# Delta-rule recurrence: the order of ScalarE's square and its copies of the second round of the block solve

## The chip, the cores and the metric

One Trainium2 chip; the program runs on one of its cores. The metric is the device time of one execution in microseconds (us), smaller is better. A core has five engines that run side by side and wait for each other by semaphores: TensorE (PE), VectorE (DVE), ScalarE (ACT), GpSimd (POOL) and SyncE (SP), the last of which only issues DMAs here.

## What is computed

A post-layer-norm transformer block on x of 4 x 2048 x 256 in float32, with 4 heads of width 64. Its attention is a gated delta rule. Cut to the part around the change:

```python
q, k = l2norm(q), l2norm(k)
v, kb = v * beta, k * beta
A = tril(-(kb @ k.T), -1)              # per chunk
T = inverse(I - A)                     # the solve
u, w = T @ v, T @ kb
for i in chunks:                       # the recurrence
    attn = causal(q_i @ k_i.T)
    u_adj = u_i - w_i @ S
    o_i = q_i @ S + attn @ u_adj
    S = S + k_i.T @ u_adj
o = p0*fir_s(v) + p1*fir_m(v) + p2*fir_l(v) + p3*o + p4*v
o = rmsnorm(o) @ Wo.T
x = layernorm(x + o)
x = layernorm(x + ffn(x))
```

## The kernel before, in words

The kernel has four stages, one after the other: `project` (projections, convolution, Gram matrices of the keys), `weights_fir` (gates, FIR filters, and the inverses of the 32-wide diagonal blocks), `delta` (the recurrence, line 792) and `ffn` (line 1451). Only `delta` is touched.

`delta` works in 16 steps (STEPS) of 128 tokens for all 4 batches, so 16 pairs of batch and head are in work at once. The 128 x 128 triangular inverse that a step needs is put together from inverses of its 32-wide diagonal blocks (`ddiag`, `tdiag`, loaded by SP) in four rounds of small matmuls. A round is four groups; each goes to one of the four PSUM banks `R`, in turn, and is taken out by a copy or an addition on another engine:

- N: TensorE multiplies `lt` by `ddiag`; ScalarE copies the result to `nmat`.
- A: `nmat` by `tdiag`; ScalarE copies it to `r1` (96 x 384 a group). VectorE subtracts `r1` from `tdiag` (term A, L1244).
- B: `nmat` by `r1`; ScalarE copies it to `r2` (64 x 256 a group). VectorE adds `r2` (term B, L1246).
- C: `nmat` by `r2`; VectorE subtracts it straight from the bank (L1261).

These rounds are run for step t+1 while step t's own recurrence goes on, and the output side (transposes T, product with Wo W, residual and layer norm) for step t-1. The result `tt` is used in step t+1 in `solve` (L1063).

The order on each engine is written out by hand; each engine takes its instructions in that order.

TensorE (`step`, from line 1094): state products X (L1051), N rounds, transposes T (L1035), attention scores Q (L1016), solve (L1063), W (L1040), outputs (L1074, L1079), state update (L1088), then A, B and C rounds (L1032).

ScalarE (`step`, from line 1181): N copies, T copies (L1161), two copies of the solution `us` (L1189), edges of `tt` (L1166), the issue of a load of raw feed-forward weights (L1171), then the square of the outputs `osq` (L1194), which waits for `mixed`, then A copies and B copies. After the step the rounded weights are made (L1177) and their store is issued (L1179).

VectorE (`step`, from line 1340): scores (L1255), a check of the rounded weights (L1334), residual (L1306), output scaling `o` (L1278), state S (L1283), mixing (L1286, signals `mixed`), head sums of `osq` (L1290, waits for the square), layer-norm statistics (L1313), term A, sums of the statistics (L1321), term B, C evacuations (L1261), right side (L1270), head normalisation (L1297), layer norm (L1327).

GpSimd takes the head sums to the power -1/2 (L1422, L1424), and the layer norm's variances (L1428, L1431). SP loads step t+2 (L916 on) once step t's state update has been done.

The first N round needs a bank that VectorE's C evacuations of the step before empty, one bank each (`bank_free`):

```python
elif not isinstance(dve0, int) or dve0:
    pe.wait_ge(dve_out, dve0 - 3 + r)
```

Step 0 has no output side (no T, W, statistics); step 15, the last, has no rounds of the solve.

Of the kernel before, what the change touches and what calls it, by code (L numbers as in the profile page):

```python
# [791 lines left out]
def delta(nc, sems, io, keep):  # L792
# [5 lines left out]
    with st.ctx:  # L798
# [91 lines left out]
        with nc.Block() as block:  # L890
# [250 lines left out]
            def arrived(eng, seq, kind, g, round0):  # L1141

                r = next(i for i, x in enumerate(seq) if x[:2] == (kind, g))
                eng.wait_ge(round_ready, round0 + r + 1)
                return R[r % 4]

            def round_base(t):
                return base(t, len)

            @block.scalar  # L1150
            def _(act):
                def copy_rounds(kind, seq, round0):
                    for g in range(2 if kind == "T" else 4):
                        bank = arrived(act, seq, kind, g, round0)
                        c = slice(g * 4, g * 4 + 4)
                        rows, cols = REGION.get(kind, (slice(0, P), slice(0, P - CH if kind == "N" else P)))
                        if kind == "T":
                            dst = oT[:, g, :].rearrange("p (b n) -> p b n", b=BATCH)
                        else:
                            dst = {"N": nmat, "A": r1, "B": r2}[kind][rows, c, cols]  # L1160
                        nc.scalar.activation(dst, bank[rows, :, cols], ACT.Copy).then_inc(act_out, 1)  # L1161

                def edges(t, p):

                    for end in (slice(0, CH), slice(P - CH, P)):
                        last = nc.scalar.activation(tt[p][end, :, end], tdiag[p][end, :, end], ACT.Copy)  # L1166
                    last.then_inc(edges_done, 1)

                def raw_weights(c):
                    act.wait_ge(w_checked, c + 1)  # L1170
                    act.dma_start(wraw[:, :], io["ffn_w"][:, bass.ds(c * WCH, WCH)]).then_inc(wraw_in, 16)  # L1171

                def round_weights(c):

                    act.wait_ge(wraw_in, c * 16 + 16)
                    act.wait_ge(w_stored, c * 16)
                    nc.scalar.activation(wround[:, :], wraw[:, :], ACT.Copy).then_inc(w_rounded, 1)  # L1177
                    act.wait_ge(w_rounded, c + 1)
                    act.dma_start(io["wr_s"][:, bass.ds(c * WCH, WCH)], wround[:, :].bitcast(f32)).then_inc(w_stored, 16)  # L1179

                def step(t, p, seq, round0, pre, tail):

                    if pre:
                        copy_rounds("N", seq, round0)
                    if tail:
                        copy_rounds("T", seq, round0)
                    for i in range(2):
                        act.wait_ge(y_ready, t * 2 + i + 1)
                        nc.scalar.activation(us[:, 4 * i:4 * i + 4, :, :], Y[i][:, :, :, :], ACT.Copy).then_inc(u_done, 1)  # L1189
                    if pre:  # L1190
                        edges(t + 1, p)
                        raw_weights(t + 1)
                    act.wait_ge(mixed, t + 1)
                    nc.scalar.activation(osq[:, :, :, :], o[:, :, :, :], ACT.Square).then_inc(sq_done, 1)  # L1194
                    if pre:
                        copy_rounds("A", seq, round0)
                        copy_rounds("B", seq, round0)

                raw_weights(0)
                copy_rounds("N", PRE, 0)  # L1200

                act.wait_ge(d_zero, 4)
                act.wait_ge(r_zero, 2)
                copy_rounds("A", PRE, 0)
                copy_rounds("B", PRE, 0)
                edges(0, 0)
                round_weights(0)
                step(0, 1, PRE, NPRE, True, False)
                round_weights(1)
                with act.Fori(0, MID // 2) as i:  # L1210
                    for j in range(2):
                        t = i * 2 + 1 + j
                        step(t, j, FULL, round_base(t), True, True)
                        round_weights(t + 1)
                t = STEPS - 1
                step(t, 0, LAST, round_base(t), False, True)
                act.wait_ge(total_ready, 1)
                nc.scalar.activation(flag[:, :], X[0][0:1, 0, 0, 0:1], ACT.Copy).then_inc(flag_done, 1)
                copy_rounds("T", LAST, round_base(t) + len(LAST))
# [700 lines left out]
```

## Time and profile before

| | |
|---|---|
| median of 3 runs | 2437.59 us (2434.59 to 2437.62) |
| the profiled execution: its own time | 2435.2 us |
| its span | 2433.3 us |
| mean granted TensorE clock | 0.956 |
| busy: PE / DVE / ACT / POOL | 89% / 51% / 37% / 24% of the span |
| ACT osq (L1194), first and last start | 664.9 and 1074.2 us, 16 of them, 1056 ns each |
| ACT copies r1 and r2 (L1161) | 632.5 to 1051.7 us, 64 of each form |

Times of rows are us from the span's start. The timeline merges neighbouring instructions of one line into one row: its start, how long the merged piece lasts, engine, line, operation, the tiles written and read, the shape of one instruction, their count, and in brackets how long the engine had been idle before it and what ended that. PE rows' ends are modelled. A granted clock of 1.00 is 2.4 GHz and 0.50 is 1.2 GHz.

### The profile page before, as it was taken

How to read it: one execution, taken by the hardware profiler on the slowest of the kernel's cores; microseconds unless marked ns; L12 is line 12 of the kernel's file. 1: busy time of each engine (PE TensorE's matmuls, PEld its weight loads, DVE VectorE, ACT ScalarE, POOL GpSimd, SP SyncE). 2: the span in 40 equal slices, each digit the busy share in tenths (PEclk: the TensorE clock that was granted, in tenths of full speed). 3: DMA queues.
4: the chain of work that ended last, by engine and by line, in shares of the span. 5: the costliest groups of instructions: out<-in, count | busy, mean ns of one | idle time of the engine just before them, and what ended most of it. 6: DMA issues, size and time to landing. Idle time of an engine off the chain costs nothing.

```text
span 2433.3 us, 40589 instructions
## 1 busy us (share of the span) xinstructions
PE 2157.0 (89%) x15412; PEld 1855.9 (76%) x15412; DVE 1235.5 (51%) x1872; ACT 895.2 (37%) x1425; POOL 593.4 (24%) x416
## 2 busy tenths in 40 slices
PE   7887865655699999967999999999999999999998
PEld 6776754555588888855888888888888888888887
DVE  5776758896477777762323332333333333323332
ACT  4554530002233334313434443444344334433442
POOL 2555555896344444430000000000000000000000
PEclk9999987887799999987999999999999999999999
DMA  3558759787989989925000000000000000000000
GB/s 131 194 197 204 194 200 211 198 207 236 241 229 249 250 235 241 254 79 219 1 18 17 0 17 17 17 0 17 17 17 0 17 17 17 0 17 17 18 1 18
DMA packets 346603, 257.53 MB, mean 106 GB/s; under 512 B 281394, under 2 KB 315698, under 8 KB 336434
## 3 DMA queue, kind: packets, MB, share of 16 engines
q1 hardware_dynamic: 333682, 232.65, 35.1%
q10 hardware_dynamic: 12864, 24.12, 2.8%
q8 instruction: 36, 0.59, 0.1%
q14 instruction: 21, 0.17, 0.0%
HBM read 156.85 MB, written 99.88 MB: 106 GB/s over the span
## 4 chain that ended last, share of the span: by engine, by line
PE 52%; issue 1%; DVE 1%; ACT 0%; DMA 0%; SPq 0%; POOL 0%; DVEq 0%; ACTq 0%; POOLq 0%
PE B L1611 46%; PE O L1639 5%; PE T L1567 1%; DVE yb L1738 0%; ACT gate L1677 0%; DMA wr<-wr_s 0%; SPq L1500 0%; DVE stats L1769 0%; ACT L1677 0%; DVE z L1764 0%; DVE z L1760 0%; DVE z L1783 0%; POOL rstd L1819 0%; SPq L1514 0%; DVEq L1733 0%
## 5 line engine op out<-in xcount | busy, mean ns | idle before, releaser
L1611 PE MATMUL B<-act1l,wr 128*128 128x512 f32 x1024 | 398.4, 389 | 0.0
L1611 PE MATMUL B<-act1h,wr 128*128 128x512 f32 x1024 | 398.3, 389 | 0.0
L1611 PE MATMUL B<-act0h,wr 128*128 128x512 f32 x1024 | 398.3, 389 | 0.0
L1611 PE MATMUL B<-act0l,wr 128*128 128x512 f32 x1024 | 398.3, 389 | 0.0
L1691 ACT ACTIVATE yb<-B,scol 128x512 f32<-128x512 f32 x256 | 176.2, 688 | 581.0 <-PE B L1611 581.0
L1726 DVE TENSOR_TENSOR act0l<-yb,act0h 128x512 fp32r<-128x512 f32 x256 | 176.1, 688 | 377.9 <-ACT act0h L1694 375.7
L1816 POOL TENSOR_TENSOR rstd<-mv,ln_eps 128x4 f32<-128x4 f32 x16 | 3.2, 199 | 1309.2 <-DVE mv L1777 1309.2
L379 DVE SCALAR_TENSOR_TENSOR acc<-proj,taps,acc 128x512 f32<-128x512 f32 x288 | 214.4, 750 | 92.3 <-ACT acc L334 83.7
L1726 DVE TENSOR_TENSOR act1l<-yb,act1h 128x512 fp32r<-128x512 f32 x128 | 88.6, 692 | 295.5 <-ACT act1h L1694 295.5
L224 PE MATMUL proj<-xt,w_qkv 128*128 128x262 f32 x768 | 195.0, 400 | 35.9 <-DMA xt<-in_xt 19.4
L1611 PEld LDWEIGHTS B<-act1h,wr 128*128 128x128 f32 x1024 | 192.2, 188 | 39.9
L1611 PEld LDWEIGHTS B<-act0h,wr 128*128 128x128 f32 x1024 | 192.2, 188 | 39.9
L1611 PEld LDWEIGHTS B<-act0l,wr 128*128 128x128 f32 x1024 | 192.2, 188 | 39.9
L1611 PEld LDWEIGHTS B<-act1l,wr 128*128 128x128 f32 x1024 | 192.2, 188 | 39.9
L1611 PE MATMUL B<-xh,wr 128*128 128x512 f32 x512 | 202.7, 396 | 11.8 <-DMA wr<-wr_s 7.6
L613 PE MATMUL conv<-toe,win 128*128 128x192 f32 x512 | 139.2, 433 | 83.1 <-DMA win<-v_s 41.8
L1611 PE MATMUL B<-xl,wr 128*128 128x512 f32 x512 | 200.8, 392 | 0.0
L613 PEld LDWEIGHTS conv<-toe,win 128*128 128x128 f32 x512 | 127.8, 316 | 94.4 <-DMA win<-v_s 43.0
L224 PEld LDWEIGHTS proj<-xt,w_qkv 128*128 128x128 f32 x768 | 141.5, 192 | 72.2 <-DVE acc L379 28.6
L1738 DVE SCALAR_TENSOR_TENSOR yb<-B,scol,gate 128x512 f32<-128x512 f32 x128 | 94.8, 750 | 183.7 <-ACT gate L1677 128.1
L783 POOL TENSOR_TENSOR two<-prods 128x256 f32<-128x256 f32 x64 | 123.6, 1932 | 17.7 <-DVE prods L725 17.7
L1611 PEld LDWEIGHTS B<-xh,wr 128*128 128x128 f32 x512 | 97.0, 189 | 37.7 <-DVE yb L1738 10.1
(164 smaller groups left out, 3477.6 us busy)
## 6 DMA issues: line engine op xcount, KB each, us to landing
qk_s<-yT SPq DMA_DIRECT2D x16, 1024.0 KB, 5.8
kk_s<-kfull SPq DMA_DIRECT2D x16, 1024.0 KB, 3.9
qk<-qk_s SPq DMA_DIRECT2D x16, 1024.0 KB, 6.7
lt<-kk_s SPq DMA_DIRECT2D x15, 1024.0 KB, 5.3
wraw<-in_ffn_w ACTq DMA_DIRECT2D x16, 704.0 KB, 6.4
wr_s<-wround ACTq DMA_DIRECT2D x16, 704.0 KB, 9.5
toe<-in_firp SPq DMA_DIRECT2D x64, 160.0 KB, 3.6
xt<-in_xt SPq DMA_DIRECT2D x16, 524.0 KB, 4.0
```

The source lines that it names most:

```text
L224: last = nc.tensor.matmul(proj[cb % 2][:, 2 * half:2 * half + 2, 0:XW], w_qkv[:, k, cb * P:cb * P + P], xt[p][:, k, 2 * half:2 * half + 2, ...
L379: nc.vector.scalar_tensor_tensor(out=acc[cb % 3][:, :, :], in0=proj[cb % 2][:, :, j:j + P], scalar=taps[:, cb, j:j + 1], in1=acc[cb % 3][: ...
L613: last = nc.tensor.matmul(conv[n % 2][:, c // 2, c % 2 * NF * WIN:(c % 2 + 1) * NF * WIN], win[h % 2][:, :, g * FCH + c], toe[part % 2][:, ...
L783: nc.gpsimd.tensor_tensor(two[n % 2][:, :, :], part[:, 0, :, :], part[:, 1, :, :], ALU.add).then_inc(two_done, 1)
L1567: last = nc.tensor.transpose(T[:, k, b * P:b * P + P], x1[p][:, b, k * P:k * P + P], ident)
L1611: last = nc.tensor.matmul(B[slot % 4][:, :], w, part, start=(k == 0 and i == 0), stop=(k == kts - 1 and i == len(parts) - 1))
L1639: last = nc.tensor.matmul(O[:, b, :], sets[0][i][:, k, b * P:b * P + P], wr[:, W3 + k * D:W3 + k * D + D], start=(k == 0 and i == 0), stop ...
L1691: last = nc.scalar.activation(dst, B[slot % 4][:, :], ACT.Gelu, scale=scol[:, slot:slot + 1])
L1726: nc.vector.tensor_tensor(sets[s][1][:, m, :], yb[n % 3][:, :], sets[s][0][:, m, :].bitcast(f32), ALU.subtract).then_inc(lo_done, 1)
L1738: nc.vector.scalar_tensor_tensor(out=dst, in0=B[(2 * m + 1) % 4][:, :], scalar=scol[:, HT + m:HT + m + 1], in1=gate[m % 2][:, :], op0=ALU. ...
L1816: nc.gpsimd.tensor_tensor(rstd[:, :], mv[:, :, 1:2].rearrange("p b o -> p (b o)"), ln_eps[:, :], ALU.add).then_inc(rs_link, 1)
```

## The change

ScalarE's A copies stand ahead of the wait for `mixed` and of the square; the B copies stay behind it. `pre` is true in steps 0 to 14.

```diff
                     if pre:
                         edges(t + 1, p)
                         raw_weights(t + 1)
+                    if pre:
+                        copy_rounds("A", seq, round0)
                     act.wait_ge(mixed, t + 1)
                     nc.scalar.activation(osq[:, :, :, :], o[:, :, :, :], ACT.Square).then_inc(sq_done, 1)
                     if pre:
-                        copy_rounds("A", seq, round0)
                         copy_rounds("B", seq, round0)
```

## Rows read from the trace of the kernel before

**Rows 1.** Page, chain that ended last, by line:
```profile
PE B L1611 46%; PE O L1639 5%; PE T L1567 1%; DVE yb L1738 0%; ACT gate L1677 0%; DMA wr<-wr_s 0%; SPq L1500 0%; DVE stats L1769 0%; ACT L1677 0%; DVE z L1764 0%; DVE z L1760 0%; DVE z L1783 0%; POOL rstd L1819 0%; SPq L1514 0%; DVEq L1733 0%
```
**Rows 2.** Timeline of PE, 863 to 896 us, one steady step and the next N:
```profile
863.94 3.81 PE L1032 MATMUL R<-ddiag,lt 128*128 128x96 f32 x32 [0.44 <-DVE tt L1261]
867.59 1.04 PE L1035 MATMUL R<-const,o 128*128 128x128 f32 x8
...
870.54 2.09 PE L1063 MATMUL Y<-x,tt 128*64 128x64 f32 x64
...
881.29 2.96 PE L1032 MATMUL R<-tdiag,nmat 128*96 128x96 f32 x32
885.67 3.18 PE L1032 MATMUL R<-r,nmat 128*64 128x64 f32 x64 [1.42 <-ACT r L1161]
...
891.26 3.81 PE L1032 MATMUL R<-ddiag,lt 128*128 128x96 f32 x32 [0.35 <-DVE tt L1261]
```
**Rows 3.** Windows: stretch, its length, busy PE, PEld, DVE, ACT, POOL, PEclk, DMA share, GB/s:
```profile
868.00:895.00 27.00, 25.18 (x375) 23.56 (x374) 19.49 (x38) 10.24 (x20) 12.60 (x7) 1.00 0.93 245
```
**Rows 4.** Timeline of DVE, 862 to 892 us:
```profile
881.40 1.40 DVE L1283 TENSOR_TENSOR S<-S,Y 64x512 f32<-64x512 f32 x2
882.84 1.22 DVE L1286 TENSOR_TENSOR o<-o,mix 128x1024 f32<-128x1024 f32 x1
885.18 1.22 DVE L1290 TENSOR_REDUCE ss<-osq 128x16 f32<-128x1024 f32 x1 [1.12 <-ACT osq L1194]
...
887.63 1.80 DVE L1244 TENSOR_TENSOR tt<-tdiag,r 96x768 f32<-96x768 f32 x2
...
890.93 0.87 DVE L1261 TENSOR_TENSOR tt<-tt,R 32x128 f32<-32x128 f32 x4
```
**Rows 5.** Timeline, 622 to 672 us, A round of the prologue:
```profile
631.51 2.93 PE L1032 MATMUL R<-tdiag,nmat 128*96 128x96 f32 x32
...
634.47 2.38 ACT L1161 ACTIVATE r<-R 96x384 f32<-96x384 f32 x5 [0.19 <-PE R L1032]
```
**Rows 6.** Timeline of ACT, the same steady step; 885.43 from a narrower stretch:
```profile
867.79 0.49 ACT L1161 ACTIVATE nmat<-R 128x384 f32<-128x384 f32 x1 [0.40 <-PE R L1032]
868.23 1.09 ACT L1161 ACTIVATE oT<-R 128x512 f32<-128x512 f32 x2
...
884.09 1.06 ACT L1194 ACTIVATE osq<-o 128x1024 f32<-128x1024 f32 x1 [9.67 <-DVE o L1286]
885.06 3.08 ACT L1161 ACTIVATE r<-R 96x384 f32<-96x384 f32 x8
885.43 1.23 ACT L1161 ACTIVATE r<-R 96x384 f32<-96x384 f32 x3
```
**Rows 7.** Timeline of DVE and PE, end of step 0 and of step 2:
```profile
670.28 0.87 DVE L1261 TENSOR_TENSOR tt<-tt,R 32x128 f32<-32x128 f32 x4
671.47 3.71 PE L1032 MATMUL R<-ddiag,lt 128*128 128x96 f32 x32
...
727.34 3.81 PE L1032 MATMUL R<-ddiag,lt 128*128 128x96 f32 x32 [1.52 <-DMA tdiag<-t_s]
```
**Rows 8.** Timeline of PE behind longer idle times, and one window (columns as rows 3):
```profile
396.26 3.80 PE L613 MATMUL conv<-toe,win 128*128 128x192 f32 x16 [2.09 <-DVE prods L725]
...
449.12 4.91 PE L613 MATMUL conv<-toe,win 128*128 128x192 f32 x16 [2.26 <-DMA toe<-in_firp]
...
450.50:453.70 3.20, 3.20 (x12) 3.10 (x11) 3.17 (x3) 0.00 (x0) 3.12 (x3) 0.50 1.22 228
...
645.18 6.94 PE L1032 MATMUL R<-ddiag,lt 128*128 128x96 f32 x32 [5.62 <-DMA tdiag<-t_s]
...
1058.12 1.97 PE L1035 MATMUL R<-const,o 128*128 128x128 f32 x8 [3.36 <-DVE o L1297]
1060.02 2.69 PE L1063 MATMUL Y<-x,tt 128*64 128x64 f32 x64
```
**Rows 9.** Tile tdiag, its DMAs from issue to landing:
```profile
DMA to landing us min/median/max: 2.4/4.3/6.9
```

## Prediction, made before the changed kernel had run

> **What bounds the kernel now.** I read the chain that ended last first. Its shares, 46% and 5% and then 1% and less, belong to lines 1567 and later, the feed-forward part [rows 1]. No line of the recurrence, in which the changed line stands, is in it, so the recurrence's bound must be read from its own timelines. It repeats itself: N rounds start at 863.94 and at 891.26, so a step is 27.32 us [rows 2], at a granted clock of 1.00 [rows 3].
>
> Follow one step. TensorE works almost without a gap from the N rounds (863.94) through the state update to the A rounds, which start right behind it (881.29): 17.35 us [rows 2]. Then VectorE has the lead: state 881.40, mixing 882.84 to 884.06, a wait of 1.12 for ScalarE's square, the head sums at 885.18, statistics, term A at 887.63, term B, and the C evacuations at 890.93 [rows 4]. The next N round starts 0.33 after the first C evacuation starts, because it needs the bank that this one empties; its 0.35 of idle time is put down to DVE tt [rows 2, 4]. So 17.35 + 9.97 = 27.32: the step is TensorE's part and VectorE's part in series, and **the square lies on the path**: VectorE is in order and stands in head_sums until it is done. TensorE's own wait for the first A copy (1.42, [rows 2]) is not on the path: without it N would still wait for the C evacuations.
>
> **The change part by part.** Nothing is added or removed. In steps 0 to 14 four A copies move ahead of the wait for the mixing and of the square; B copies stay behind it. No DMA issue is moved past anything but the square and the A copies: the raw-weight load is issued before both, the rounded-weight store after both. Step 15 has no A round.
>
> *When the copies can run.* The A matmuls start at 881.29 and take 2.96 [rows 2]. The fourth copy cannot start before its group is done. In the prologue the copies follow TensorE directly: matmuls from 631.51, fourth copy at 634.47, 2.96 later [rows 5]. So here 881.29 + 2.96 = 884.25 (884.29 with the 0.04 of the fourth N copy, 867.79 against 863.94 + 3.81 [rows 2, 6]).
>
> *When the square runs.* It now follows that copy. Queued A copies start 0.37 apart (885.06, 885.43), an N copy and the next one 0.44 (867.79, 868.23) [rows 6]. That puts the square at 884.62 to 884.73 against 884.09 now, which is just behind the mixing's end [rows 4, 6]. **The delay is 0.53 to 0.64; I take 0.59**, between the two, since the last A copy is like the first row in shape and like the second in having just waited.
>
> *What it costs on the path.* Everything in VectorE's queue from the head sums on starts 0.59 later. Terms A and B don't wait: the A copies end by 884.8 and the B copies, as worked out below, by 887.1, both before term A alone begins (887.63 and 0.59). Nothing on VectorE gets shorter, so the C evacuations and N are 0.59 later. Behind the last changed step there is no N; there TensorE's transposes (1058.12) wait for the normalisation (DVE o L1297), which stands in the same queue [rows 8]. GpSimd's power and the later layer norm move along with VectorE.
>
> *What TensorE gains.* B starts right behind A, 1.42 earlier. The B copies wait for the square: first at about 884.66 + 0.97 = 885.63 (the present spacing of square and first copy [rows 6]), last done near 887.1, which leaves the C rounds and the state products about 1.4 earlier than now. They are worth nothing: the gap ahead of N becomes 0.35 + 1.42 + 0.59 = 2.36, in one piece. The cover of that gain is the C evacuation; if it went, TensorE would be next.
>
> *Two steps differ.* In step 0 there is no statistics work, and N (671.47) begins 1.19 after the C evacuation (670.28), right behind the state products [rows 7]. There the products come earlier, and N starts at 670.28 + 0.59 + 0.33 = 671.20: a gain of 0.27. In step 2 N waited 1.52 for the diagonal blocks' DMA, 1.17 more than the usual 0.35 [rows 7]; that hides 0.59. The load is issued after the state update, which doesn't move. So 15 changed steps make 13 x 0.59 - 0.27 = **7.4 us**.
>
> *Contention.* The A copies now read PSUM while VectorE adds the state and mixes; no row shows the two side by side. The low end is 0. For the high end let them take turns, with the mixing late by four whole copies, 4 x 0.37 = 1.5 a step, from the spacing above. I take 0: the nearest rows are the present A copies beside the head sums, which take 1.22, the same as the mixing with nothing beside it [rows 4, 6].
>
> *The clock.* A gap of 2.36 is longer than any in the steady stage. Elsewhere, after 2.09 idle the convolution's 16 matmuls took 3.80 (237 ns each), after 2.26 idle 4.91 (307 ns each), and the granted clock behind the latter was 0.50, its lower level of 1.2 GHz. After 3.36 idle TensorE's rows are longer too: transposes 1.97 and solve 2.69, where the steady step has 1.04 and 2.09, 0.93 + 0.60 = 1.53 lost [rows 2, 8]. After 5.62 idle N took 6.94 for 3.81, 3.13 lost [rows 2, 8]. So a fall costs 1.53 to 3.13 on TensorE's part, which is on the path. The low end of the number of falls is 0 (behind 1.52 N took its usual 3.81, [rows 2, 7]), the high end 13. At 2.36, just over the gap that fell, I take 5 of 13 at 1.53, the row nearest to the gap: **7.6 us**.
>
> The Trainium skill (TensorE: Matmul & The Clock Gate, "What's actually happening") says that the slow clock is the default and that activity alone releases it. By that rule gathering two short pauses into one long one speaks against this change, and the sum would be 15.0; by the gaps of 2.09 and less alone it would be 7.4.
>
> **Sum.** The profiled execution took 2435.2 (span 2433.3 and 1.9 around it). 2435.2 + 7.4 + 7.6 = 2450.2. The median of the runs, 2437.59, is 2.4 above that execution, so the forecast is 2452.6.
>
> **Rivals.** About 0.2% (4.9 us) is what a measurement of this kernel can tell from no change.
>
> (a) *No fall of the clock.* 7.4 alone: 2445.0. For it: 2.09 did nothing. Against: 2.26 did.
>
> (b) *The clock falls in every step.* 13 x 1.53 + 7.4 = 27.3: 2464.9; at 3.13 each 48.1: 2485.7. For it: the gap is the same in each step. Against: it lies between a row that kept the clock and one that lost it.
>
> (c) *Not slower: the DMA of the diagonal blocks is the real gate of N.* It is issued behind the state update, in several parts, and each takes 2.4 to 6.9 to land, median 4.3 [rows 9], while N starts 9.97 behind the update [rows 2]. A step in which it lands 0.59 or more behind the C evacuation hides the delay; from 5 further such steps on the total of (a) is under 4.9, and with all 13 it is 2437.3. Against: 0.33 from evacuation to N in the steady steps, and only step 2 shows a DMA. The same result would come if the copies didn't hold up the square at all, that is if the fourth A group were done by 883.7; the prologue's 2.96 speaks against it.
>
> (d) *Faster.* TensorE's 1.4 would count if N did not wait for VectorE. All 13 together would be 18 less, 2419. The 0.33 speaks against it.
>
> **How the numbers follow.** Some falls 0.44, none 0.28, nearly all 0.18, (c) 0.08, (d) 0.02. The first case spans 2446 to 2464. The range 2443 to 2470 takes in (a) with its 0.53 to 0.64 (6.6 to 8.0, some 1.5 of scatter between runs) and the cheap half of (b); outside are (c), (d) and the dear half of (b). Faster 0.02, same 0.08, slower 0.90.
>
> **What would show it.** Right: ACT osq starts about 0.6 after DVE's mixing ends, and DVE's wait for it grows from 1.12 to about 1.7; TensorE's wait of 1.42 ahead of B is gone and the one ahead of N is near 2.4, put down to DVE tt; undisturbed steps of 27.9; a clock under 1.00 in some of the steps, with N, T or Q rounds longer there. Wrong: a square at 884.1 behind the A copies, a wait for N put down to DMA in most steps, a step that shrinks. If the clock stays at 1.00 everywhere, the second term falls; if it falls in every step, the count was too small.

## The result and the profile after

| | before | changed |
|---|---|---|
| median | 2436.09 us (2431.0 to 2437.62, 4 runs) | 2461.06 us (2453.03 to 2461.6, 4 runs) |
| profiled execution / its span | 2435.2 / 2433.3 us | 2461.6 / 2459.8 us |
| ratio to before | | 1.0098, 95% interval 1.0072 to 1.0125 |

The changed kernel is slower by 1.0%, some 24 us, with the forecast at 2452.6 and the range from 2443 to 2470. Run once more beside others (`after_again`, below) its ratio was 1.0097 (1.0082 to 1.0113). Lines below the edit have moved by one: L1290 of before is L1291 after, and the square is L1196.

The page of the changed kernel, its heading and the granted clock in the 40 slices:

```profile
span 2459.8 us, 40589 instructions
PE 2172.0 (88%) x15412; PEld 1869.0 (76%) x15412; DVE 1241.5 (50%) x1872; ACT 899.6 (37%) x1425; POOL 583.0 (24%) x416
...
PEclk9999977887799999997999999999999999999999
```

The same number of instructions, and TensorE busy for 15 us more (2157.0 before): the same matmuls took longer. The page can't say which. The windows view over the middle of the recurrence can. Its columns are those of [rows 3]; first the kernel before, then the changed one:

```profile
680.00:1040.00 360.00, 334.82 (x4910) 313.58 (x4906) 264.35 (x498) 137.57 (x263) 164.55 (x93) 1.00 0.94 241
```
```profile
680.00:1040.00 360.00, 328.79 (x4664) 308.66 (x4664) 253.63 (x465) 131.16 (x246) 147.04 (x87) 0.96 0.90 228
```

In the same 360 us 246 fewer TensorE instructions were done, at a granted clock of 0.96 in place of 1.00. So there are two things: TensorE stands idle for longer in each step, and its clock is slower for part of the time. The timeline of one step, and of the N round behind it, TensorE first, answers to [rows 2]:

```profile
899.90 2.96 PE L1032 MATMUL R<-tdiag,nmat 128*96 128x96 f32 x32
902.79 3.30 PE L1032 MATMUL R<-r,nmat 128*64 128x64 f32 x64
906.29 2.02 PE L1051 MATMUL X<-S,qk 128*128 128x128 f32 x16 [0.20 <-issue]
910.58 3.81 PE L1032 MATMUL R<-ddiag,lt 128*128 128x96 f32 x32 [2.27 <-DVE tt L1262]
...
938.60 5.44 PE L1032 MATMUL R<-ddiag,lt 128*128 128x96 f32 x32 [2.51 <-DVE tt L1262]
```

The 1.42 ahead of the B round is gone, and the pause ahead of N has grown from 0.35 to 2.27 and 2.51, still put down to VectorE's C evacuations. The step, from N round to N round, is 938.60 - 910.58 = 28.02 for 27.32. And the second N took 5.44 for 3.81. VectorE and ScalarE in the same step answer to [rows 4, 6]:

```profile
900.01 1.40 DVE L1284 TENSOR_TENSOR S<-S,Y 64x512 f32<-64x512 f32 x2
901.45 1.23 DVE L1287 TENSOR_TENSOR o<-o,mix 128x1024 f32<-128x1024 f32 x1
904.49 1.22 DVE L1291 TENSOR_REDUCE ss<-osq 128x16 f32<-128x1024 f32 x1 [1.82 <-ACT osq L1196]
...
910.25 0.87 DVE L1262 TENSOR_TENSOR tt<-tt,R 32x128 f32<-32x128 f32 x4
```
```profile
902.89 0.49 ACT L1161 ACTIVATE r<-R 96x384 f32<-96x384 f32 x1 [0.19 <-PE R L1032]
903.40 1.06 ACT L1196 ACTIVATE osq<-o 128x1024 f32<-128x1024 f32 x1
904.37 1.16 ACT L1161 ACTIVATE r<-R 64x256 f32<-64x256 f32 x4
```

The fourth A copy starts 2.99 after the A round, the square 0.51 after that, and VectorE waits 1.82 for it where it waited 1.12: **0.70 late**. From the head sums on VectorE does what it did before: C evacuation 5.76 after the head sums (5.75 before), N 0.33 after that. And the granted clock in a window inside that second N round (938.60 to 944.04), 0.50:

```profile
940.60:943.80 3.20, 3.20 (x17) 3.20 (x17) 2.17 (x5) 0.98 (x2) 0.00 (x0) 0.50 1.04 400
```

In this way N rounds of 5.43 or 5.44 stand in 6 of the steps and one of 6.80 in a seventh:

```profile
734.59 5.43 PE L1032 MATMUL R<-ddiag,lt 128*128 128x96 f32 x32 [3.27 <-DMA tdiag<-t_s]
879.57 6.80 PE L1032 MATMUL R<-ddiag,lt 128*128 128x96 f32 x32 [2.51 <-DVE tt L1262]
```

A step that begins with a long N is 29.65, one that begins with a normal N 28.02: a fall costs 1.63. The one of 6.80 begins a step of 31.01: 2.99. In the six cases of 5.43 or 5.44 the clock went down 1.1 to 1.9 us after N had started; in the one of 6.80 it was at 0.50 already when N started. The length of the pause doesn't tell which N will be long: of the six pauses of 2.51 two are followed by a long N, of the five of 2.27 three.

**The sum of the profile.** To keep what comes before the recurrence out, I take the stretch from the N round of the second solve (645.18 before, 649.76 after) to the transposes of the last step (1058.12 and 1084.88): 412.94 and 435.12, 22.2 more. It comes apart as 13 steps x 0.70 = 9.1 (all but steps 0 and 2); the falls 6 x 1.63 + 2.99 = 12.8; step 2, at whose end a DMA gates N, 0.6 beyond its fall; step 1 0.4 beyond its 0.70; step 0 shorter by 0.6. That is 22.3. The entry itself lay at 643.5 to 650.1 in the fourteen profiles, in no order that follows the change (649.76 and 643.71 in two profiles of the changed kernel), and I take it for scatter.

### The profile page after: what moved, and what is told of

Read it like the earlier page. It is cut to its first block, busy times and chain, and to the rows that moved or that the text cites. A ratio compares the mean times of both kernels' runs of the same rounds, so it can differ in the third digit from the quotient of the medians.

```text
span 2459.8 us, 40589 instructions
## 1 busy us (share of the span) xinstructions
PE 2172.0 (88%) x15412; PEld 1869.0 (76%) x15412; DVE 1241.5 (50%) x1872; ACT 899.6 (37%) x1425; POOL 583.0 (24%) x416
## 4 chain that ended last, share of the span: by engine, by line
PE 51%; issue 1%; DVE 1%; ACT 0%; DMA 0%; SPq 0%; POOL 0%; DVEq 0%; ACTq 0%; POOLq 0%
PE B L1612 46%; PE O L1640 5%; PE T L1568 1%; DVE yb L1739 0%; ACT gate L1678 0%; DMA wr<-wr_s 0%; SPq L1501 0%; DVE stats L1770 0%; ACT L1678 0%; DVE z L1765 0%; DVE z L1761 0%; DVE z L1784 0%; POOL rstd L1820 0%; SPq L1515 0%; DVEq L1734 0%
## 5 line engine op out<-in xcount | busy, mean ns | idle before, releaser
L1032 PE MATMUL R<-ddiag,lt 128*128 128x96 f32 x512 | 78.4, 326 | 68.3 <-DMA tdiag<-t_s 39.5
L1032 PEld LDWEIGHTS R<-ddiag,lt 128*128 128x128 f32 x512 | 75.8, 239 | 71.6 <-DVE tt L1262 36.6
```

Of the source, the lines that this page charges most:

```text
L1032: last = nc.tensor.matmul(out, left, right, start=True, stop=True)
```

## Experiments

Two terms were to be told apart, and rivals that name the DMAs. Every run was timed against the kernel before on its chip; "stretch" is the length defined above (412.9 before, 435.1 changed).

### Fill the pause: fill16, fill8, fill4

The edit on TensorE, with n = 16, 8 and 4:

```diff
                     from_state(t, p)
+                    if seq is FULL:
+                        for j in range(n):
+                            nc.tensor.matmul(Y[1][:, j % 4, :, :], ident, ident, start=True, stop=True)
                     run("N", *rest)
```

> The changed kernel with 16 matmuls of 128x128 added on TensorE between the state products and the N rounds of steps 1 to 14 (their results go to a free bank and are read by nobody). They take about 2.05 us and fit in the wait of 2.27 to 2.51 ahead of N. Theory (two terms: the square is 0.70 late on VectorE in each step; the one long pause lets the clock fall, 7 times in the profile, 12.8 in all): steps of 28.02, granted clock 1.00 throughout steps 1 to 13, N always 3.81; the second term goes and the first stays, about 2436.1 + 13 x 0.70 = 2445. Rival (the loss is late DMAs or contention, and the clock only goes along with it): TensorE is as late as before, 2461 or above. Rival (the pause is no pause, N is held by TensorE itself): each step longer by 2, about 2489.

Measured: 2471.66, ratio 1.0139 (1.0122 to 1.0156). I had mis-sized the filler. One of these float32 matmuls is two instructions in the trace, and 16 of them take 3.74, not 2.05:

```profile
875.09 3.74 PE L1100 MATMUL Y<-const 128*128 128x128 f32 x32
878.66 3.60 PE L1032 MATMUL R<-ddiag,lt 128*128 128x96 f32 x31
```

N comes without any wait (the row shows 31 of its 32 instructions), TensorE gates it, and the steps from the third on are 28.81 to 29.06. The 2445 of the theory was missed; the rival's 2461 or above is met, but by the filler's length and not by what the rival named. The run doesn't weigh the terms, though it shows what was wanted of the clock: there is no fall in steps 1 to 14, and every N has its normal length. The run with 8 was the one that fitted.

> As the run with 16, with 8 such matmuls, about 1.05 us, so that a pause of 1.2 to 1.5 is left ahead of N. Theory: the kernel before has pauses of 1.42 and 1.52 without a fall, so the clock stays at 1.00 here too: again about 2445. If any pause beside the shorter work before it lets the clock fall, some falls stay and the time lies between 2445 and 2461.

Measured: 2447.17, ratio 1.0042 (1.0029 to 1.0055), stretch 421.3:

```profile
866.79 1.95 PE L1100 MATMUL Y<-const 128*128 128x128 f32 x16
869.47 3.81 PE L1032 MATMUL R<-ddiag,lt 128*128 128x96 f32 x32 [0.72 <-DVE tt L1265]
```
```profile
680.00:1040.00 360.00, 350.95 (x5045) 330.38 (x5046) 269.36 (x489) 136.53 (x256) 151.52 (x91) 1.00 0.93 234
```

Steps 1 to 13 are 28.02 (28.01 to 28.03), the clock is 1.00. The pauses left are 0.23 to 0.72, shorter than the 1.2 to 1.5 of the expectation, so what it says of such pauses is not tested here. TensorE does more work than in the changed kernel and the program is 14 us faster. This parts the loss: about 10 us (7 to 13) is the late square, the rest, 13.6 by the two ratios, went with the long pause. By their intervals the 13.6 has some 7 us either way (13.4, and 5 either way, with `after_again` below). The falls counted in the profile come to 12.8.

> The changed kernel with 4 matmuls ahead of N (two rows of the trace each, about 1.0 us by the 1.95 that 8 took), which leaves a pause of 1.2 to 1.5. Theory: no fall of the clock with such a pause, steps of 28.02, the same 2447 as with 8. Rival (any pause that stands alone ahead of N lets the clock fall): falls in some steps, 2450 to 2460.

Measured: 2452.57, ratio 1.0072 (1.0059 to 1.0086). A miss for the theory as I had put it. The pauses left are 1.38 and 1.62, one of 2.60 by a DMA, and three N rounds are long, each behind a pause of 1.62:

```profile
818.06 5.44 PE L1032 MATMUL R<-ddiag,lt 128*128 128x96 f32 x32 [1.62 <-DVE tt L1265]
875.73 3.81 PE L1032 MATMUL R<-ddiag,lt 128*128 128x96 f32 x32 [1.62 <-DVE tt L1265]
```

So a pause as short as 1.62 can do it here, in 3 of 7 cases, and a fall costs the same 1.63. The 1.52 of [rows 7] was one case and proved less than I took from it. The three falls are 4.9; the medians of this run and of the one with 8 differ by 5.4. That these agree is in part chance, for the two profiles differ by 9.7 in the stretch (431.0 and 421.3), and 4.8 of that is no fall behind a pause: a slower clock in step 0 (1.9), a wait of 1.56 for DMA qk in step 1, and the wait of 2.60 in step 2.

### Undo the late square alone: three_first

ScalarE takes three A copies ahead of the square and the fourth behind it:

```diff
                     if pre:
-                        copy_rounds("A", seq, round0)
+                        copy_rounds("A", seq, round0, range(3))
                     act.wait_ge(mixed, t + 1)
                     nc.scalar.activation(osq[:, :, :, :], o[:, :, :, :], ACT.Square).then_inc(sq_done, 1)
                     if pre:
+                        copy_rounds("A", seq, round0, range(3, 4))
                         copy_rounds("B", seq, round0)
```

> Three of the four A copies ahead of the square, the fourth behind it. The third group is done at about 2.2 into the A round, and its copy's slot ends as the mixing does. Theory: the square is not late (VectorE's wait for it is 1.12 again), steps of 27.32, the first term is gone; TensorE still runs early, with a pause of about 1.8 ahead of N. With no fall at 1.8: 2435 to 2437, same as the kernel before. Rival (TensorE's early B and C rounds and the pause alone cost the time): falls in several steps, N of 5.4 in them, 2436 + 1.6 each, up to 2450. Rival (the copies beside VectorE's state and mixing slow these down): VectorE's rows L1284 and L1287 above 1.40 and 1.23.

Measured: 2442.84, ratio 1.0025 (1.0016 to 1.0035), stretch 418.3; the time expected, 2435 to 2437, missed. The first term is gone as expected:

```profile
917.26 0.49 ACT L1161 ACTIVATE r<-R 96x384 f32<-96x384 f32 x1 [0.19 <-PE R L1032]
917.77 1.06 ACT L1196 ACTIVATE osq<-o 128x1024 f32<-128x1024 f32 x1
918.73 1.68 ACT L1161 ACTIVATE r<-R 96x384 f32<-96x384 f32 x5
```
```profile
918.86 1.22 DVE L1292 TENSOR_REDUCE ss<-osq 128x16 f32<-128x1024 f32 x1 [1.14 <-ACT osq L1196]
```

VectorE's wait is 1.14, and eight of the steps are 27.33 or 27.34. VectorE's mixing and state take 1.22 and 1.40 beside the copies, so there is no contention that these rows show. But it isn't quite the kernel before. Its pause is 1.71 to 1.84, without a fall behind any of those, and two N rounds, where a DMA or a late evacuation had made the pause 3.31 and 2.31, are long. Two falls are 3.3 of its 5.3 in the stretch, and step 1 is 1.6 longer, in which TensorE waits for the load of q and k:

```profile
678.06 2.06 PE L1016 MATMUL R<-qk 64*128 64x128 f32 x32 [1.58 <-DMA qk<-qk_s]
```

### Both terms away: three_fill4

Three copies first, and the 4 matmuls.

> Three A copies ahead of the square, and 4 matmuls in TensorE's pause ahead of N. Both terms of the loss are taken away: the square is not late, the pause is about 0.8. Theory: steps of 27.33, no fall of the clock, the time of the kernel before, 2434 to 2438. Rival (TensorE's early start costs something by itself, the DMAs say): above 2440 with a clock of 1.00.

Measured: 2442.26, ratio 1.0026 (1.0016 to 1.0035), stretch 418.2; the 2434 to 2438 expected missed. Eleven N rounds have pauses of at most 0.94 and ten steps are 27.34, but the N rounds of steps 2 and 3 wait 1.94 and 1.96 for the diagonal blocks, and both are long, 5.27 to the transposes for 3.65. A third fall lies in step 0 (668.5 to 672.5). So neither the theory nor the rival fits whole: the time is the rival's, above 2440, but the clock was not at 1.00 throughout. The two long N rounds alone are 3.3 of the 5.2 that its stretch has over the kernel before. What precedes both is a wait for a DMA, so I looked at the DMAs. The tile view of qk shows a difference, the load of q and k from issue to landing, first before, then the changed kernel:

```profile
DMA to landing us min/median/max: 5.6/6.7/7.6
```
```profile
DMA to landing us min/median/max: 5.5/7.4/8.3
```

In the changed kernel ScalarE is done with its copies earlier. It converts the raw weights and issues their store 6.93 after the A round starts (906.83 against 899.90), where it was 8.14; in this run it is 6.76. The guess is that those 704 KB now move beside the loads.

### The layer-norm statistics first: stats_first, before_stats_first

VectorE's statistics go ahead of the head sums, into the wait for the square:

```diff
                     outputs(t, p)
-                    head_sums(t)
                     if tail:
                         spread(t - 1, 1 - p, dve0 + used(seq, "dve", 1 + next(i for i, x in enumerate(seq) if x[:2] == ("W", 1))))
+                    head_sums(t)
```

> The changed kernel with VectorE's layer-norm statistics (1.39) moved ahead of the head sums, into its wait of 1.82 for the square. Theory (VectorE's chain sets when N starts): the wait shrinks to about 0.43, steps 28.02 - 1.39 = 26.63, the pause ahead of N about 1.0, no fall of the clock: 2436.1 - 13 x 0.69 = about 2427. Rival (something else gates N, the DMA of the diagonal blocks): N waits for DMA tdiag in most steps and the time stays above 2434.

Measured: 2435.47, ratio 0.9995 (0.9984 to 1.0007), where about 2427 was expected. VectorE's wait shrank to 0.50 and A to N from 10.68 to 9.39, so the chain does set N, and N waited for DMA tdiag only in steps 0 and 3, not in most steps as the rival had it. But the steps came out at 26.7 to 27.6, not 26.63, with two waits for DMA qk of up to 0.54 ahead of the scores, and one fall behind the DMA wait of 3.44 in step 3. Next, the same edit on the kernel before.

> The kernel before with only VectorE's statistics moved ahead of the head sums, into its wait of 1.12 for the square. Theory: VectorE's chain loses 1.12, but TensorE's state products end 0.35 ahead of the present N, so TensorE gates N: steps of about 26.95, 2436.1 - 14 x 0.37 = about 2431. Rival (the DMAs of a step, the scores' and the diagonal blocks', are the next gate at about 27.1, as in the run stats_first): waits for DMA qk or tdiag on TensorE, 2433 to 2436.

Measured: **2425.18, ratio 0.9963 (0.9951 to 0.9975)**, faster than both, stretch 402.9:

```profile
882.15 2.02 PE L1051 MATMUL X<-S,qk 128*128 128x128 f32 x16
884.01 3.71 PE L1032 MATMUL R<-ddiag,lt 128*128 128x96 f32 x32
```

N follows the state products without a wait, in steps of 26.62 to 26.80. The gain is 9 by the ratio where 5 was expected: the A round to N is 9.46 here (874.55 to 884.01) and 9.97 before. The wait of 0.35 is gone, and N, which no longer has to wait, starts 0.16 before the row ahead of it has ended (884.01 against 882.15 + 2.02; ends of PE rows are modelled). A step of 26.7 also refutes the rival that the DMAs hold it at 27.1. With ScalarE's order as it was they don't.

### Is it the earlier store? stats_first_late, three_fill4_late, after_late, before_late

A copy of 848 elements to a spare tile holds ScalarE 0.8 longer ahead of the conversion:

```diff
+                    nc.scalar.activation(spare[:, :], wraw[:, 0:848], ACT.Copy)
                     nc.scalar.activation(wround[:, :], wraw[:, :], ACT.Copy).then_inc(w_rounded, 1)
```

> The run stats_first with a copy of 848 elements, read by nobody, on ScalarE ahead of the conversion of the raw weights: the rounded weights' store is issued about 0.8 later (7.7 behind the start of the A round, where the kernel before has 8.14 and the changed one 6.93). Theory (a third term: the change lets ScalarE issue this 704 KB store 1.2 earlier, beside the loads of the diagonal blocks and of q and k, which then land later, 7.4 for 6.6): the load of q and k lands sooner, TensorE's waits for it mostly go, steps of about 26.8, 2426 to 2431 where stats_first took 2435.5. Rival (the store has nothing to do with it): 2435 again.

> The run three_fill4 with the same copy ahead of the weights' conversion. That run had neither a late square nor, in the middle steps, a fall of the clock, and yet took 2442.3, with its first steps held up by DMA. Theory (the earlier store is what is left): 2436 to 2439. Rival (the store has nothing to do with it): 2442 again, with N of steps 1 and 2 waiting for DMA tdiag by 1.9.

> The changed kernel with the same copy ahead of the weights' conversion. Theory: of its 21 to 25 only the DMA term goes, 2 to 4: 2454 to 2458; the clean steps stay at 28.02 and the falls of the clock stay. If the falls came from late DMAs, they would go as well, and the time would be near 2445.

> The kernel before with the same copy, as a control: ScalarE has the room for it (it waits 3.0 for the N round), and the store, issued at about 8.9 for 8.14, moves further from the loads. Theory: the same as before or up to 2 faster, 2434 to 2437. If the copy itself cost something, this run would be slower.

| run | median | ratio (95%) | without the delay | load qk, median |
|---|---|---|---|---|
| stats_first_late | 2434.74 | 0.9992 (0.9983 to 1.0001) | 0.9995 | 6.7, was 7.3 |
| three_fill4_late | 2441.04 | 1.0022 (1.0012 to 1.0032) | 1.0026 | 6.8, was 7.4 |
| after_late | 2457.44 | 1.0088 (1.0075 to 1.0101) | 1.0098, 1.0097 | 6.6, was 7.4 |
| before_late | 2435.55 | 0.9993 (0.9984 to 1.0002) | 1 | 5.6, was 6.7 |

The load's part of the guess is borne out: in all four the load lands sooner. In the profile of stats_first_late nine of the ten last steps are 26.73 to 26.75 (the tenth 26.90), where stats_first had 26.74 to 27.56, and in after_late the N at the end of step 2 no longer waits for the diagonal blocks (it waits 2.08 for DVE tt). The price in time is another matter. The first two expectations missed (2426 to 2431 and 2436 to 2439), and there the rival, that the store has nothing to do with the time, did as well. Every ratio moved the expected way, by 0.0003 to 0.0010, and each is inside the other's interval. So **the earlier store makes the load land later; delaying it gave back 0.7 to 2.4 us in the ratios, which these runs can't tell from nothing**. What keeps three_fill4 above the kernel before isn't settled. In three_fill4_late the N rounds of steps 2 and 3 still wait 1.80 and 2.20 for DMA tdiag, the second with a fall. Why the first steps are hit, and in some variants (three_first, three_fill4, stats_first, with the delay and without, and fill4) and hardly in fill8, stays open.

after_late settles one more thing. Six of its N rounds are long, of 5.44 each, those of steps 2, 4, 7, 9, 12 and 14, and all six stand behind a wait for DVE tt. So a late DMA isn't needed for a fall of the clock.

### The changed kernel again: after_again

> The changed kernel once more, beside the others of this call and in more runs. Theory: clean steps of 28.02 and falls of the clock in N rounds, whose number differs from execution to execution (7 in the first profile), so that runs scatter more than those of the kernel before: 2450 to 2465, median near 2460. If the number of falls is fixed by the program, the profile shows 7 again and the runs scatter as little as before.

Measured: 2457.12 (2455.71 to 2462.91), ratio 1.0097. In its profile the same seven N rounds are long as in the first, those of steps 2, 3, 5, 7, 8, 10 and 13, with the longest in step 8, though the recurrence was entered 6.0 earlier (643.71). So in two executions the falls came in the same steps, and the runs of the changed kernel reach from 2453.0 to 2462.9, which is no wider than those of the kernel before (2431.4 to 2440.9 in 29 runs). Both speak for the second alternative of the expectation, a number of falls that the program fixes. A small edit moves them: in after_late, with its copy of 0.8 on ScalarE, six falls came in other steps. Two profiles are too few to say more.

## Why the prediction was right, and where its sizes were off

- *The square is on the path, and VectorE's chain sets N.* Shown: VectorE's rows behind the square are unchanged and N is 0.33 after the C evacuation [rows 2, 4]. Taking the delay away with three copies first gave 27.34 again; shortening the chain with the statistics moved N ahead.
- *The delay of 0.59 (0.53 to 0.64).* It measured 0.70, outside its bounds. The fourth copy started at 2.99 behind the A round, 2.96 to 3.00 were taken. The spacing to the square was the mis-sized part: 0.51 where I took 0.37 to 0.44. The copy takes 0.49, so the square did not overlap with it, while both spacings that I had to choose from were shorter than the copy [rows 6]. Why is not shown: the N copy there had waited too and was overlapped. The first term was 7.4 by the text. By the steps it is 9.1, by fill8's time 10.2 (7.1 to 13.4).
- *TensorE's 1.4 is worth nothing, the pause becomes 2.36.* It became 2.27 and 2.51 in turn and gave nothing.
- *The clock, 5 falls at 1.53 = 7.6.* Right in kind; the term was too small in both factors: 7 falls, six at 1.63 and one at 2.99, 12.8. fill8, with the pause filled, gave back 13.6. The 5 was a choice between 0 and 13, not worked out, so that it came near 7 is in part luck. And its ground, that gaps of 2.09 and less kept the clock and one of 2.26 lost it, doesn't hold as a bound: it fell behind 1.62 (fill4) and held behind four of the six pauses of 2.51. The Trainium skill (TensorE: Matmul & The Clock Gate, "What's actually happening") says that activity releases the slow clock. This case agrees: with added, useless matmuls the granted clock of the stage was 1.00 for 0.96, and the kernel was faster.
- *Step 0 gains 0.27, step 2 hides the delay.* Step 0 was 25.67 for 26.29, but the gain of 0.27 was not there: the N round that begins it took 5.69 for 6.94, at a clock still low in both, which I take for scatter (3.8 to 7.1 in the fourteen profiles), and the N at its end was gated by a DMA (1.84). Without the first N the step was 0.6 longer. Step 2 hid nothing: it was longer by 0.6 beyond its fall, since the DMA that gates its end came later itself. The step at fault is "No DMA issue is moved past anything but the square and the A copies": true of the order, but the store moved in time. after_late, where that wait is gone in step 2, supports this; it is one profile, and the wait in step 0 is still there (1.92).
- *Contention on PSUM: 0.* Right: mixing and state took 1.23 and 1.40 beside the copies, 1.22 and 1.40 before.
- *The rivals.* No fall (a), which would have been 2445.0, fell with the profile, and fill8 shows its case, at 2447. Falls in every step (b) was too much. A hidden delay (c) and faster (d) fell with N's waits: in steps 1 to 14, 12 of them are put down to DVE tt, two to a DMA.

The sum of the text, 15.0 over the profiled execution, should have been 9.1 + 12.8 and some. The path, the wait and the sign were right; both terms were too small, the second most.

## What to carry to other kernels

An instruction that another engine stands waiting for goes ahead of copies whose reader gains nothing by having them earlier; an idle time on TensorE that isn't on the path (its 1.42 here) is no reason to reorder. When reordering gathers TensorE's short waits into one, read the granted clock of the stage, and price a fall from a row of it: here it more than doubled the loss. And look at the wait itself: work that is already in the waiting engine's queue, put into it, was worth 0.37%, more than any order of the copies.

## What the runs showed of the hardware that was not expected

- The granted clock fell behind 3 of the 7 pauses of 1.62 (fill4), behind none of the seven of 1.83 or 1.84 (three_first), and behind 2 of the 6 of 2.51 in the changed kernel; the length of the pause alone doesn't decide.
- 8 added matmuls a step that compute nothing made the changed kernel 14 us faster (medians of 2461.06 and 2447.17).
- One float32 matmul of 128x128 is two matmul instructions of the trace, and 8 of them took 1.95, 16 took 3.74.
- A falling clock costs N 1.63 in nearly every case (5.43 or 5.44 for 3.81), and 2.99 once, where the clock was down before N began.
